# Latent attention of a two-layer kernel: query blocks projected transposed, rotated in that layout and spread over partitions by DMA

## The reference, cut to what matters

```python
q = rms_norm(x @ wq_a.T, q_norm_w) @ wq_b.T            # rank 192, then 32 heads x (128 + 64)
q_nope, q_pe = q[..., :128], rope(q[..., 128:])        # interleaved pairs, 64 wide
kv = x @ wkv_a.T; kv_c, k_pe = kv[..., :64], rope(kv[..., 64:])
kv_up = rms_norm(kv_c, kv_norm_w) @ wkv_b.T            # 32 heads x (128 + 128)
scores = (q_nope @ k_nope.T + q_pe @ k_pe.T) / sqrt(192)   # causal, softmax
out = (probs @ v) @ wo.T
```

## Time and profile before

| | us |
|---|---|
| median of 3 runs | 2440.08 (2437.95 to 2443.78) |
| span of the profiled execution | 2443.6 |
| PE busy | 2218.4 (91%) |
| DVE busy | 1442.6 (59%) |
| ACT busy | 1132.7 (46%) |
| POOL busy | 690.4 (28%) |
| this stage, first key projection to last output projection | about 1338 to 1982 |

### The profile page before, as it was taken

The page is one execution under the profiler, slowest core; times in us unless marked ns, Lnnn a source line. Parts: engine busy times, 40 slices in busy tenths (PEclk is TensorE's granted clock), DMA queues, the critical chain, the costliest instruction groups (busy, mean ns, idle before and its releaser), DMA issues. The chain is left out here.

```text
span 2443.6 us, 34377 instructions
## 1 busy us (share of the span) xinstructions
PE 2218.4 (91%) x11952; PEld 1531.9 (63%) x11952; DVE 1442.6 (59%) x2655; ACT 1132.7 (46%) x2735; POOL 690.4 (28%) x872
## 2 busy tenths in 40 slices
PE   6999998869999999999987799999999986899988
PEld 4344466656777777776765566766766764654457
DVE  5777574336665655655636555555555555657756
ACT  4666643224444444444435455555555533325553
POOL 2000001544444444444430111211111111336621
PEclk8899999989999999999998899999999997979999
DMA  2000022741111011111001100000000011443310
GB/s 86 1 1 1 21 87 86 165 100 52 31 39 52 31 39 53 31 40 35 14 35 61 38 32 32 1 32 32 32 32 1 21 48 39 149 97 72 73 35 35
DMA packets 93729, 113.84 MB, mean 47 GB/s; under 512 B 36644, under 2 KB 51364, under 8 KB 91384
## 3 DMA queue, kind: packets, MB, share of 16 engines
q1 hardware_dynamic: 45560, 73.37, 9.1%
q0 software_dynamic: 48000, 38.28, 6.6%
HBM read 84.23 MB, written 27.26 MB: 46 GB/s over the span
## 5 line engine op out<-in xcount | busy, mean ns | idle before, releaser
L1842 POOL TENSOR_TENSOR attn0b_probs<-attn0b_probs,attn0b_recip 128x128 f32<-128x128 f32 (+3 forms) x256 | 192.6, 773 | 223.4 <-DVE attn0b_recip L2081 223.2
L2477 ACT ACTIVATE attn1a_probs<-attn1a_scores,attn1a_negmax 128x128 f32<-128x128 f32 (+3 forms) x256 | 132.8, 523 | 175.2 <-DVE attn1a_negmax L2594 175.1
L1948 ACT ACTIVATE attn0b_probs<-attn0b_scores,attn0b_negmax 128x128 f32<-128x128 f32 (+3 forms) x256 | 132.8, 524 | 150.0 <-DVE attn0b_negmax L2074 148.9
L1956 ACT ACTIVATE attn0b_probsT<-attn0b_turned 128x128 f32<-128x128 f32 (+3 forms) x128 | 56.0, 438 | 243.0 <-PE attn0b_turned L2222 242.6
L1468 DVE TENSOR_REDUCE attn0a_negmax<-attn0a_by_query 128x2 f32<-128x1024 f32 x128 | 152.3, 1219 | 21.6 <-PE attn0a_by_query L1555 21.6
L2235 PE MATMUL attn0b_out<-attn0b_probsT,attn0b_v_now 128*128 128x512 f32 x320 | 153.8, 611 | 10.3 <-DVE attn0b_probsT L2088 10.3
L2407 POOL TENSOR_TENSOR attn1a_q_tok<-attn1a_part_a,attn1a_part_b 128x256 f32<-128x256 f32 x64 | 47.2, 737 | 349.7 <-DVE attn1a_part_b L2619 349.7
L2594 DVE TENSOR_REDUCE attn1a_negmax<-attn1a_scores 128x2 f32<-128x256 f32 (+3 forms) x128 | 105.6, 825 | 52.3 <-PE attn1a_scores L2803 50.4
L2074 DVE TENSOR_REDUCE attn0b_negmax<-attn0b_scores 128x2 f32<-128x256 f32 (+3 forms) x128 | 104.8, 819 | 47.2 <-PE attn0b_scores L2211 47.2
L2815 PE MATMUL attn1a_turned<-ident_f,attn1a_probs 128*128 128x128 f32 x640 | 114.2, 276 | 17.9 <-DVE attn1a_probsT L2602 16.2
L37 PE MATMUL attn0b_aux<-attn0b_wo_hi,attn0b_oT_hi 128*128 128x512 f32 x256 | 125.7, 491 | 1.4 <-DVE attn0b_oT_lo L2092 1.4
(11 more groups left out here) (509 smaller groups left out, 6305.5 us busy)
## 6 DMA issues: line engine op xcount, KB each, us to landing
pre<-in_b_o SPq DMA_DIRECT2D x16, 1024.0 KB, 5.6
pre<-in_b_q SPq DMA_DIRECT2D x8, 1024.0 KB, 6.6
pre<-in_b_kv SPq DMA_DIRECT2D x5, 1024.0 KB, 6.3
attn0b_vals<-attn0b_v_out SPq DMA_DIRECT2D x16, 256.0 KB, 4.9
attn0b_keys_hi<-attn0b_part_hi POOLq DMA_DIRECT2D x32, 128.0 KB, 4.8
attn0b_keys_lo<-attn0b_part_lo POOLq DMA_DIRECT2D x32, 128.0 KB, 7.3
attn0b_v_now<-attn0b_vals SPq DMA_DIRECT2D x16, 256.0 KB
attn0b_kT_hi<-attn0b_keys_hi POOLq DMA_DIRECT2D x16, 256.0 KB, 3.2
```

The lines of the kernel that those rows point to most:

```text
L1842: pool.tensor_tensor(x, x, recip[:, r % 2, e:e + 1].broadcast_to([P, (qt + 1) * P]), ALU.mult).then_inc(s_scaled, 1)
L1948: act.activation(probs[:, r % 2, e, 0:width], scores[r % 2][:, e, 0:width], ACT.Exp, bias=negmax[:, r % 2, e:e + 1], accum_out=sums[:, r % ...
L2477: act.activation(probs[:, r % 2, e, 0:width], scores[r % 2][:, e, 0:width], ACT.Exp, bias=negmax[:, r % 2, e:e + 1], accum_out=sums[:, h % ...
```

## The change: what it does

The query projection is turned around. The weights are now the stationary operand and the latents of one whole batch (512 tokens) the moving one, so that a **block** is 128 query dimensions by 512 tokens. A turn has eight blocks: for each batch four kinds, which are the first and the second 32 of each pair's rotary halves for four heads (kinds 0 and 1), and the latent dimensions of two heads (kinds 2 and 3). The host lays the weights out for that. The 64 last query latents take up both halves of a 128-row block: the host doubles the weight rows, and DVE writes the low half of the latents into rows 64 to 127 of the high tensor, so two matmuls stand for the products of that part, and a block has five matmuls.

Rotation happens on whole blocks: DVE multiplies each of the kinds 0 and 1 by a cos and a sin table (four instructions a batch, 128 x 512), POOL subtracts and adds (two instructions), ACT writes the high halves and POOL the low halves into a slot of the new tile `stage` (three slots). Kinds 2 and 3 are copied by ACT (high) and DVE (low) into a slot. SP then spreads each slot to `qT` with DMAs of both halves: four of 32 partitions for kinds 0 and 1, two of 64 partitions for kinds 2 and 3. A spread waits until the turn before has scored that batch, and a slot is written again once its spread has landed. The score matmuls wait for the spreads once a batch.

The early fills lie elsewhere: C blocks in even rounds (16i - 12 to 16i + 2), W at 16i - 14; Q is gone, and odd rounds have no C. SP loads the next turn's query weights before it spreads, and the output weights between the two batches. The softmax scale is taken into the query norm weights by one small POOL instruction; the zeroing of weight rows is gone.

```diff
+    KINDS = 4
+    BLOCKS = BATCH * KINDS
+    SLOTS = 3
+    OF_KIND = (2, 3, 0, 1)
+    SPREADS = (G, G, 2, 2)
     for i in range(TURNS):
+        for u in range(BLOCKS):
+            early[PER * i - 12 + 2 * u] = [("C", i, u)]
         for t in range(TILES):
-            early[PER * (i - 1) + 7 + 2 * t] = [("C", i, t)]
-            early[PER * (i - 1) + 8 + 2 * t] = [("Q", i, t)]
             late[PER * i + 15 + 2 * t] = [("E", i, t)]
-        late[PER * (i - 1) + 6] = [("W", i, 0), ("W", i, 1)]
+        late[PER * i - 14] = [("W", i, 0), ("W", i, 1)]
         late[PER * i + 14] = [("G", i, 0), ("G", i, 1)]
...
+            def spread_out(i, u):
+                b, kind = divmod(u, KINDS)
+                block = BLOCKS * i + u
+                sp.wait_ge(s_qhi, block + 1)
+                pairs = BATCH * i + b
+                if kind < 2:
+                    sp.wait_ge(s_rotlo, 2 * pairs + kind + 1)
+                else:
+                    sp.wait_ge(s_latlo, 2 * pairs + kind - 1)
+                if i >= 1:
+                    sp.wait_ge(s_scores, PER * (i - 1) + PAIRS * QT * (b + 1))
+                into, done_by = qT[:, :, :, bass.ts(b, SEQ)].bitcast(F32), s_spread[block % SLOTS]
+                of = stage[:, block % SLOTS, :, :].bitcast(F32)
+                if kind < 2:
+                    rows = slice(LAT + 32 * kind, LAT + 32 * kind + 32)
+                    for j in range(G):
+                        sp.dma_start(into[rows, :, j, :], of[32 * j:32 * j + 32, :, :]).then_inc(done_by, 16)
+                else:
+                    for e in range(2):
+                        sp.dma_start(into[0:LAT, :, 2 * (kind - 2) + e, :],
+                                     of[LAT * e:LAT * (e + 1), :, :]).then_inc(done_by, 16)
...
+            def add_rotated(i, b):
+                at = BATCH * i + b
+                pool.wait_ge(s_rope, 4 * at + 4)
+                pool.tensor_tensor(by_cos[:, 0, :], by_cos[:, 0, :], by_sin[:, 1, :], ALU.subtract).then_inc(s_padd, 1)
+                pool.tensor_tensor(by_sin[:, 0, :], by_sin[:, 0, :], by_cos[:, 1, :], ALU.add).then_inc(s_padd, 1)
...
+            def slot_free(block):
+                if block >= SLOTS:
+                    act.wait_ge(s_spread[block % SLOTS], spread_until(block - SLOTS))
+
+            def rotated_hi(i, b):
+                for kind in range(2):
+                    block = BLOCKS * i + KINDS * b + kind
+                    act.wait_ge(s_padd, 2 * (BATCH * i + b) + kind + 1)
+                    slot_free(block)
+                    act.activation(stage[:, block % SLOTS, 0, :], rotated(kind), ACT.Copy).then_inc(s_qhi, 1)
+
+            def latent_hi(i, u):
+                block = BLOCKS * i + u
+                act.wait_ge(s_c, block + 1)
+                slot_free(block)
+                act.activation(stage[:, block % SLOTS, 0, :], aux[FILL["C", i, u] % 2][:, :], ACT.Copy).then_inc(s_qhi, 1)
...
+            def rotate(i, u):
+                b, kind = divmod(u, KINDS)
+                at = BATCH * i + b
+                dve.wait_ge(s_c, BLOCKS * i + u + 1)
+                if at >= 1:
+                    dve.wait_ge(s_rotlo, 2 * at)
+                x = aux[FILL["C", i, u] % 2][:, :]
+                dve.tensor_tensor(by_cos[:, kind, :], x, cos_q[:, :], ALU.mult).then_inc(s_rope, 1)
+                dve.tensor_tensor(by_sin[:, kind, :], x, sin_q[:, :], ALU.mult).then_inc(s_rope, 1)
...
-            def project_queries(i, t):
-                aux_free(("C", i, t))
-                if t == 0:
+            def project_queries(i, u):
+                b, kind = divmod(u, KINDS)
+                into, x = aux[FILL["C", i, u] % 2][:, :], OF_KIND[kind]
+                aux_free(("C", i, u))
+                if u == 0:
                     pe.wait_ge(s_wlo, 2 * i + 2)
                     pe.wait_ge(s_rlo, 2 * i + 2)
-                for k in range(2):
-                    last = mm3(pe, aux[FILL["C", i, t] % 2][:, :], pair(latT_hi, latT_lo, slice(None), k, bass.ts(t, P)),
-                               (wq_hi[:, k, :, :].rearrange("p g x -> p (g x)"),
-                                wq_lo[:, k, :, :].rearrange("p g x -> p (g x)")), start=k == 0, stop=k == 1)
-                last.then_inc(s_c, 1)
-
-            def turn_queries(i, t):
-                aux_free(("Q", i, t))
-                pe.wait_ge(s_clat, i * TILES + t + 1)
-                pe.wait_ge(s_padd, i * TILES + t + 1)
-                for j in range(G):
-                    last = pe.transpose(aux[FILL["Q", i, t] % 2][:, bass.ts(j, P)], q_tok[:, t % 2, j, :], m.ident[:, :])
-                last.then_inc(s_q, 1)
+                mm3(pe, into, pair(wq_hi, wq_lo, slice(None), 0, x), pair(latT_hi, latT_lo, slice(None), 0, bass.ts(b, SEQ)),
+                    start=True, stop=False)
+                both = latT_hi[:, 1, bass.ts(b, SEQ)]
+                pe.matmul(into, wq_hi[:, 1, x, :], both, start=False, stop=False)
+                pe.matmul(into, wq_lo[:, 1, x, :], both, start=False, stop=True).then_inc(s_c, 1)
...
-                pe.wait_ge(s_qlo, i * TILES + t + 1)
+                if pr == 0 and qt == 0:
+                    for slot in range(SLOTS):
+                        pe.wait_ge(s_spread[slot], spread_until(last_in_slot(BLOCKS * i + KINDS * (b + 1) - 1, slot)))
```

More of the change, by code:

```diff
@@ L2296, in place, with spread_until, last_in_slot @@
         return i, b, pr, qt, r // QT
+    def spread_until(block):
+        return sum(16 * SPREADS[x % KINDS] for x in range(block % SLOTS, block + 1, SLOTS))
+    def last_in_slot(block, slot):
+        return block - (block - slot) % SLOTS
     with ExitStack() as ctx:
@@ L2377, in _ @@
                 sp.dma_start(wo_in[:, :, :], d["b1_o"][i]).then_inc(s_ino, 16)
+            def spread_out(i, u):
[19 more added lines that the diff above has]
+                                     of[LAT * e:LAT * (e + 1), :, :]).then_inc(done_by, 16)
+            load_queries(0)
+            load_outputs(0)
+            for i in range(TURNS):
+                if i + 1 < TURNS:
+                    load_queries(i + 1)
+                for u in range(KINDS):
+                    spread_out(i, u)
+                if i >= 1:
+                    load_outputs(i)
+                for u in range(KINDS, BLOCKS):
+                    spread_out(i, u)
             sp.wait_ge(s_w, 2 * TURNS)
@@ L3466, in shape_constants @@
     cos, sin = np.cos(ang), np.sin(ang)
-    scale = np.float32(1.0 / np.sqrt(np.float32(192.0)))
     both, signed = np.concatenate([cos, cos], 1), np.concatenate([-sin, sin], 1)
-    c["b1_cos_q"], c["b1_sin_q"] = tiles(both * scale), tiles(signed * scale)
+    c["b1_cos_q"], c["b1_sin_q"] = [np.tile(x.T, (4, 1)).astype(np.float32) for x in (cos, sin)]
     c["b1_cos_k"], c["b1_sin_k"] = tiles(both), tiles(signed)
```

200 lines of the change are left out of this document (88 added, 112 removed).

## The result

| | before | after |
|---|---|---|
| median of 4 runs beside each other, us | 2440.26 (2437.95 to 2443.78) | 2405.47 (2401.97 to 2413.68) |
| ratio, 95% interval | | 0.9855 (0.9835 to 0.9874) |
| span of the profiled execution, us | 2443.6 | 2400.3 |

The kernel is 34.8 us faster. The forecast was 2398, with a range of 2386 to 2418. The changed kernel run again later, beside other runs of the kernel before, took 2402.91 (ratio 0.9819, 0.9794 to 0.9845).

What follows compares the result with a forecast made beforehand. PE was taken to set the pace. Six turns -38.7, last turn -4.5, first turn -2.6, lead-in +2.5 and clock +1.0 sum to -42.3 us; from the median 2440.1 that gives 2398, range 2386 to 2418.

Steps and rivals of the forecast that it cites:

- theory A of the experiments: Experiments' hypothesis: gain is PE work removed from steady rounds; the missing 6 us lost before first G, mainly to clock.
- PE sets the pace, and bare rounds tell what a round costs without its fill: Mid-stage: PE bounds; 512-, 128-, 256-, 384-rounds become 4.57, 3.93, 3.80, 3.85 us, a quad 1.15 us less.
- A turn of 68.6: Steady turns: each loses 6.45 us, from 75.0 to 68.6; six turns 38.7 us less.
- the push by rotation: 128-rounds: DVE's rotation delays the 256-round's maximum by 0.4 us, with a 1.45 us projection still before the transposes.
- Spreads at nothing, with 2.7 to 4.4 us of slack: Steady rounds: spreads land before ACT needs the slot again, so they cost nothing; rival of late landing, chance 0.04.
- The lead-in +2.5: First C to first score: scores wait for block 3 of batch 0, +1 to +4 us, taken as +2.5.
- The first turn -2.6 and the clock +1: First turn: rounds with neither C nor E save 2.6 us; low clock at first scores costs 1.
- The way to the first block: nothing: Prelude before the first block: one small DVE instruction a tile gained, zeroing lost, so 0 us.
- The last turn -4.5: From the seventh turn's G round to the last G round, counted round by round: 4.5 us less.
- PE did not gain all its work: Rival: all removed PE work (43 us) is gained and waits shrink too, -55 us, 2385; chance 0.08.
- ACT's tight spot at the rotated high halves: ACT has 0.5 us slack before copying the second head's `probsT`; rival without it: 19 us lost, 2417, chance 0.16.
- The exchange was not for nothing: Rival: DVE and ACT hold the quad at 17.3 us, or DMA traffic stretches matmuls; 2440, chance 0.03.

Runs made afterwards that it cites:

- two_slots: Changed kernel with two slots of the stage tile instead of three: 2481.32 us, ratio to before 1.0169.
- own_place: Changed kernel with block 3 of the first turn written to unused output-tile columns instead of a slot: 2405.14 us, ratio to before 0.9836.
- two queues: Changed kernel, blocks re-placed by measured round prices, ACT issuing the first turn's spreads of blocks 2 and 3, block 3 in its own place: 2389.53 us, ratio 0.9760.
- sixth_matmul: Changed kernel with the first matmul of every block issued twice, six a block: 2421.98 us, ratio to before 0.9915.
- keep_warm: Changed kernel with unread matmuls added where PE only waits, before the rounds and in the first turn: 2402.38 us, ratio to before 0.9831.
- the repetition: The changed kernel itself, unedited, run again later beside other runs of the kernel before: 2402.91 us, ratio 0.9819.
- transposes_back: Changed kernel with four fp32 transposes of 128 columns, later overwritten, ahead of every block: 2420.05 us, ratio to before 0.9893.
- thin_spreads: Changed kernel with every spread DMA from the second turn on moving 64 of its 512 columns: 2403.81 us, ratio to before 0.9849.

## Why the prediction was right, and where it was off

The prediction was right in direction, mechanism and size. It erred by 6.2 us of the stage's 42.3, and by 7.5 in the time: counted from round to round, 1.8 on the way to the first block, 0.3 in the lead-in, 1.9 in the first turn, 2.4 in six steady turns, and -0.3 from there to the end. So theory A of the experiments was half right: 4.0 us are lost ahead of the first G round, but the steady rounds have a share, and the clock is only part of it.

1. *PE sets the pace, and bare rounds tell what a round costs without its fill.* Right. Forecast 4.57, 3.93, 3.80, 3.85; measured 4.59, 3.91, 3.79 or 4.02, 3.78. The two parts of the gain are shown by putting them back: 64 matmuls and 256 transposes cost 1.62 and 2.65 us a turn, 4.3 of the 6.1 that a turn lost. The rest is argued from the bare rounds.
2. *A turn of 68.6.* 68.98 measured, 2.4 us over six turns. Two terms were too small. The W round is 6.04, not 5.75. Its second half starts 4.95 us into the round as before, so the wait was read rightly, but it now computes 128 rows (1.10 us in the row above, 0.68 in the earlier trace rows), which the count of fills left out. Two of the four 256-rounds are 0.22 longer, with 0.16 of wait behind DVE's division, in rounds that follow a rotated block: the push by rotation that I named and took as covered by the projection. The G round was 5.77 (5.9).
3. *Spreads at nothing, with 2.7 to 4.4 us of slack.* Right for three slots: ACT stands on a slot once, in the lead-in. two_slots shows that a late microsecond costs its full length and slightly more (rounds longer by 4.4 to 6.5 for waits of 4.0 to 5.1). The landings of 2.7 to 4.6 in the earlier trace rows were misread as DMAs within SBUF; they write to a tensor in DRAM. The spreads themselves landed in 2.4 and 3.7. Door 1 of the page SBUF — State Buffer in the Trainium skill had the layout reach half of the ports, by an estimate from its figures 2.4 us instead of 1.2 for the 512 KB of a block. The runs bear it out, as far as they go: the first spreads move at 203 to 225 GB/s with the DMA engines busy all the time (windows above), which for 512 KB is 2.3 to 2.6 us. No run has a layout that reaches more ports. It changed nothing in the steady turns, as said, but in the lead-in the transfers are what the first score waits for, and whether a faster layout would shorten it no run shows.
4. *The lead-in +2.5.* Measured +2.8, but not by the mechanism that I wrote first: the slot of block 3 held ACT for 4.8 us, and when it didn't (own_place) the first score was as late. With two queues 0.6 to 1.5 us come back; the rest lies behind transfers that keep the DMA engines busy. That +2.5 came out is in part luck. (PE was idle there for 30% of the time before, not for half.)
5. *The first turn -2.6 and the clock +1.* Together +0.3 to the G round instead of -1.6. **The term that was mis-sized is the clock.** It was down at the first scores, as forecast (0.50 until 1387), and then fell a second time, between 1400 and 1401, for 6 us. That second fall cost 2.5 us by itself (5.18 and 3.64 against 3.92 and 2.38 in sixth_matmul; 2.1 to 2.6 by keep_warm); what the first one cost, no run separates. Without the second fall the rounds are 2.2 us shorter than before, and 2.3 in the repetition, where it cost 1.3, near the -2.6 of the forecast. But that number was partly luck. Added up by its own terms, with four 128-rounds and a 384-round at +0.8 and the W round moved, the first turn comes to -1.5; the 128-rounds then grew by only 0.33 to 0.49 where the clock was up, while the 512-rounds lost 0.66 and not 0.5. The page TensorE: Matmul & The Clock Gate (Part 1) of the Trainium skill says that the clock falls after idling, and the prediction had it make +3 likelier. The traces agree in part: the clock fell behind waits of PE in the changed kernel and stayed up where PE was kept busy (0.97 over the stretch of keep_warm), but in sixth_matmul and transposes_back it stayed at 1.00 through the same waits of 1.54 and 0.88 us.
6. *The way to the first block: nothing.* It was +1.8. I costed the added DVE instruction and the zeroing, and overlooked that the two tables for the queries grew from 128 to 256 KB each and stand first in the queue that the first key rotation waits for. The wait is shown, its share of the 1.8 is not.
7. *The last turn -4.5.* -4.7 from round to round.

The rivals: PE did not gain all its work (that would be a turn below 67). ACT's tight spot at the rotated high halves held: no wait of PE for the second head's copy in a steady turn. The exchange was not for nothing, and the bytes of the spreads cost nothing in steady turns (thin_spreads).

## What to carry to other kernels

Read what a round costs with and without a fill, for each kind of round, also those that carry something else: the prices found here (0.73 to 1.7 us for the same five matmuls) made the six steady turns 7.6 us shorter, and left-out rounds (W, G) were the main reason why an expectation missed by 24. Where a schedule is moved, look at the first pass of the pipeline apart from the steady one, since it lacks fills that the steady one has. Where two kernels are compared by an instruction inside a round, check that the same work stands ahead of it in both; here that moved 0.8 us from one stretch to another. A buffer count that hides a DMA's landing is worth counting through: from three slots to two was 76 us, and a place of its own for block 3 of the first turn, the one wait left, brought nothing.

## What the runs showed of the hardware

- A DMA within SBUF of 16 KB takes 1.8 us to land and one of 128 KB 2.4, so below that the part that doesn't grow with the size dominates. SP issues one every 0.6 us in steady turns and every 0.66 to 0.85 in the lead-in, and up to 2.0 us apart where two queues issue at once.
- Twelve such DMAs of 2.1 MB together, between 32 or 64 partitions, ran at 203 to 225 GB/s with the 16 DMA engines busy throughout; 256 KB landed every 1.2 to 1.3 us though issued every 0.7. A second queue to issue them made little difference (0.6 to 1.5 us).
- The granted clock fell to 0.50, the lower level of 1.2 GHz, some 17 to 18 us after the first score, with no wait of PE longer than 1.54 us since its clock had come back, and returned 6 us later. In the repetition of the same program it fell in the same round and came back a round earlier; in sixth_matmul and transposes_back, with the same waits, it did not fall.
- The start of the stage lay within 1326.90 to 1342.09 us over fourteen profiles with the same instructions ahead of it. An effect below 5 us in this kernel has to be read from a stretch, not from the whole.
